# The filler of a double step moved between its two score steps, in the second half of an attention and feed-forward kernel

## The reference, cut to what matters

```python
x = x + layernorm(attn(layernorm(x)))      # x: (16, 2048, 1024), 16 heads of 64
x = x + layernorm(ffn(layernorm(x)))
# attn: q = x@Wq+bq; k = (x@Wk+bk)@Wl+bl; v = (x@Wv+bv)@Wl+bl
#       softmax(q k^T / 8) v, heads joined, @ Wo + bo
# ffn:  x@base_W^T + base_b + shared low-rank pair (16)
#       + 6 routed low-rank pairs (16 each), weighted by a top-2 gate of softmax(x@router_W^T + router_b)
```

## Time and profile before

| | |
|---|---|
| median of the runs of before | 1413.39 us (1412.29 to 1520.67, 3 runs) |
| profiled execution | 1412.82 us |
| its span, slowest core (core 4) | 1411.3 us |
| the other cores' spans | 1407.9 to 1410.2 us |
| mean granted clock of core 4 | 0.989 |
| PE busy | 1317.9 us, 93% of the span |
| ACT busy | 1042.0 us, 74% |
| DVE busy | 705.3 us, 50% |
| POOL busy | 433.5 us, 31% |

### The profile page before, as it was taken

The page is one execution under the profiler, slowest core; times in us unless marked ns, Lnnn a source line. Parts: engine busy times, 40 slices in busy tenths (PEclk is TensorE's granted clock), DMA queues, the critical chain, the costliest instruction groups (busy, mean ns, idle before and its releaser), DMA issues.

```text
span 1411.3 us, 43965 instructions; the slowest of 8 cores (1407.9 to 1411.3 us)
## 1 busy us (share of the span) xinstructions
PE 1317.9 (93%) x17392; PEld 818.0 (58%) x17392; DVE 705.3 (50%) x1679; ACT 1042.0 (74%) x1138; POOL 433.5 (31%) x598
## 2 busy tenths in 40 slices
PE   6899999999999999999998999989999999998883
PEld 2456666666666666665555655555555555555551
DVE  0562434323332323232335676677777667667665
ACT  0367777777777777777777888878888888887651
POOL 5220101000010100000004555555556555465633
PEclk9999999999999999999999999999999999999997
DMA  9950112202020110123852212321222221222011
GB/s 131 232 162 6 54 30 73 64 17 59 15 62 19 47 43 26 25 78 92 113 114 64 77 59 72 121 71 60 77 78 82 91 77 45 86 69 86 23 62 45
DMA packets 67129, 98.90 MB, mean 70 GB/s; under 512 B 30208, under 2 KB 43904, under 8 KB 66416
## 3 DMA queue, kind: packets, MB, share of 16 engines
q1 hardware_dynamic: 56944, 83.03, 19.5%
q0 software_dynamic: 9984, 13.06, 6.8%
HBM read 76.56 MB, written 32.57 MB: 77 GB/s over the span
## 4 chain that ended last, share of the span: by engine, by line
PE 76%; DVE 7%; issue 5%; ACT 5%; DMA 3%; POOL 2%; DVEq 0%; SPq 0%; POOLq 0%; ACTq 0%
PE fb L379 34%; PE sc L1122 17%; PE av L1154 15%; ACT p_sb L1139 4%; PE fb L431 4%; DMA wvT_sb<-wvT 2%; DVE gt L896 1%; PE sc L379 1%; DVE x L812 1%; PE fb L853 1%; DMA xst<-x 1%; PE fb L776 1%; PE sc L1124 1%; POOL wl_sb L67 1%; PE fb L324 1%
## 5 line engine op out<-in xcount | busy, mean ns | idle before, releaser
L1139 ACT ACTIVATE p_sb<-sc 128x1024 bf16<-128x1024 f32 x1024 | 991.0, 1021 | 261.3 <-PE sc L1124 258.2
L1154 PEld LDWEIGHTS av<-v_sb,p_sb 128*128 128x128 bf16 x8192 | 320.8, 97 | 97.1 <-issue 2.3
L1122 PE MATMUL sc<-q_sb,k_sb 64*128 64x256 bf16 (+1 forms) x2176 | 330.6, 265 | 16.0 <-ACT p_sb L1139 14.5
L1154 PE MATMUL av<-v_sb,p_sb 128*128 128x65 bf16 x8192 | 340.1, 193 | 0.5 <-issue 0.5
L1124 PE MATMUL sc<-q_sb,k_sb 64*128 64x256 bf16 (+1 forms) x2176 | 332.8, 266 | 0.0
L1122 PEld LDWEIGHTS sc<-q_sb,k_sb 64*128 64x128 bf16 x2176 | 149.6, 94 | 82.8 <-issue 46.8
L266 POOL TENSOR_SCALAR rsa<-sta 128x1 f32<-128x1 f32 x32 | 7.3, 227 | 523.9 <-DVE sta L261 357.4
L1124 PEld LDWEIGHTS sc<-q_sb,k_sb 64*128 64x128 bf16 x2176 | 146.3, 94 | 0.0
L379 PE MATMUL fb<-wo_sb,ut 128*128 128x512 bf16 x496 | 136.1, 381 | 4.9 <-DVE gt L890 3.3
L379 PE MATMUL fb<-bw_sb,x3fm 128*128 128x512 bf16 x480 | 135.6, 383 | 1.0 <-DVE x3fm L251 0.9
L379 PE MATMUL fb<-xfm,wq_sb 128*128 128x512 bf16 x512 | 129.5, 381 | 0.0
(11 more groups left out here) (172 smaller groups left out, 1478.5 us busy)
## 6 DMA issues: line engine op xcount, KB each, us to landing
xst<-x SPq DMA_DIRECT2D x64, 512.0 KB, 5.2
out<-y_sb SPq DMA_DIRECT2D x31, 512.0 KB, 3.1
urow<-u_scr SPq DMA_DIRECT2D x30, 256.0 KB, 5.2
u_scr<-u SPq DMA_DIRECT2D x64, 64.0 KB, 2.1
q_scr<-kq SPq DMA_DIRECT2D x32, 128.0 KB, 2.5
q_sb<-q_scr SPq DMA_DIRECT2D x4, 1024.0 KB, 8.3
u_scr<-u_sb SPq DMA_DIRECT2D x7, 512.0 KB, 3.6
wkT_sb<-wkT POOLq DMA_DIRECT2D x8, 256.0 KB, 11.6
```

What stands on the lines that cost most here:

```text
L1122: t.matmul(sc[slot][:, ci * w:(ci + 1) * w], k_sb[0:64, j, c * 128:(c + 1) * 128], qa[0:64], start=True, stop=True, tile_position=(0, 0))
L1139: exp_tok[g] = P.op("S", lambda a: a.activation(ps[:], sc[slot][:], AF.Exp, bias=-SHIFT, scale=1.0), tok, av_tok.get(g - 4))
L1154: r = t.matmul(av[u % 2][:, o:o + 65], ps[:, p0:p0 + 128], v_sb[:, j, c * 130 + h * 65:c * 130 + (h + 1) * 65], start=(s == 0 and h == 0 a ...
```

## The change

In the turns of the second half the scores of step 2m+1 are issued after the filler of the turn and ahead of P·V, where before they directly followed those of step 2m. In the first half nothing changes. No instruction is added or taken away; which quanta a turn takes is the same.

```diff
             qk(2 * m)
-            qk(2 * m + 1)
+            if m < NM // 2:
+                qk(2 * m + 1)
             rate = rate_of(m)
             credit = min(credit + rate, 1.6 * rate)
             while filler and credit > 0 and (filler[0][2] is None or filler[0][2]()):
                 credit -= pop()
+            if m >= NM // 2:
+                qk(2 * m + 1)
             if m > 0:
                 pv(2 * m - 2)
                 pv(2 * m - 1)
```

## The result

| | before | after |
|---|---|---|
| median | 1412.84 us | 1432.9 us |
| profiled execution | 1412.82 us | 1432.76 us |
| its slowest core, span | 1411.3 us (core 4) | 1431.2 us (core 5) |
| median span of die 0, die 1 | 1409.0, 1410.1 us | 1429.7, 1427.3 us |

The ratio is 1.0143, 95% interval 1.0129 to 1.0157: +20.1 us where +15.4 us were forecast.

A forecast was written before the change was run, and what follows sets the result against it. TensorE was taken to pace the second half, losing time to scores waiting for ScalarE. Seams of 48.1 us less 32.7 us of waits gave +15.4 us on 1412.82, forecast as 1428 us, 1.1% slower, range 1408 to 1443.

The forecast's parts named there:

- Part 1: Second half: the second score step's wait for ScalarE's exponential goes, 126 places, 32.7 us gained.
- slack of 0.72 us: After the change, the next double step's second scores want their tile 0.72 us after its exponential has freed it.
- Part 2: Second half: two more half-row/full-row passages on TensorE per double step, 0.19 us in each of 253, 48.1 us lost.
- Part 3: Waits of the filler's matmuls, 29.9 us in 26 waits before: net change taken as zero.
- The one example at the loop's start: Passage from filler to scores at 112.02 to 112.33 us, used to price it at 0.31 us, 0.09 us lost.
- the bounds of -6 and +8.8: Limits in us on the change in the filler's waits, by whether their release hangs on earlier filler or on P·V.
- A: Rival: passages cost nothing because scores' weight loads are fetched under the running filler; 1380 us, chance 0.04.
- D: Rival: the scores' wait on ACT comes back behind the filler, so nothing is gained; 1461 us, chance 0.04.
- B: Rival: the filler's waits shrink by half of 29.9 us as turns become more even; 1413 us, chance 0.13.
- C: Rival: VectorE is late for the filler after a unit's end, 24.5 us at most; 1437 to 1453 us, chance 0.12.
- the forecast's case: The main forecast of 1428 us, given as 1417 to 1439 us in the list of chances, chance 0.65.
- What the profile would show: L1122's wait nearly gone, passages 0.31 and 0.21 us, `fb` rows 24 to 39 us, ACT's exponentials standing singly.

The follow-up runs named there:

- both_halves: The changed kernel with the second score step placed behind the filler in the first half too: 1484.7 us, ratio to before 1.0507.

## Why the prediction was right

*Part 1, the wait goes: 32.7 us.* Right in mechanism and size. With exponentials of half length the kernel before falls by 32.7 us, and the tally puts 34.0 us within the scores. The slack of 0.72 us behind the change held: 1.6 us of waits are left, and cheaper exponentials give the changed kernel nothing.

*Part 2, two seams more: 48.1 us.* Right in mechanism, and a little low. Over the first half, where the filler hardly waits, the lines with seams grow by 50.3 us, 0.20 us a turn where 0.19 was said. Between the two kernels with halved exponentials the same five lines go from 233.3 to 278.9 us, 45.6 us; but the line from scores to filler holds the wait of the filler's first matmul too, and it falls by 4.3 us, so the other four give 49.9. The single passages are as priced: in the kernel after the median from a filler matmul of 512 columns to scores is 0.31 us, and from scores to P·V 0.20. The one example at the loop's start was enough to price a passage that occurs nowhere in the second half of the kernel before.

*The term that was missing: P·V itself, 3.3 us.* The prediction took P·V as one block whose inside does not change. From its first start to its last a block of 16 takes 469 ns behind filler and 479 ns behind scores (medians, the same in either half of the loop). The 10 ns lie in the first two distances, on average 29.7 and 33.6 ns before, 38.6 and 35.9 after; the other 13 stay within 0.4 ns. That fits with the weight loads. In the kernel before they start at 903.78, 0.21 us ahead of P·V's 903.99, while filler still runs; in the kernel after they start together with P·V, at 922.73. That this makes the 10 ns is an argument from the two timelines; no run tested it by itself.

```profile
903.78 0.75 PEld L1154 LDWEIGHTS av<-v_sb,p_sb 128*128 128x128 bf16 x16
903.99 0.66 PE L1154 MATMUL av<-v_sb,p_sb 128*128 128x65 bf16 x16
```

Some 2.6 of the 3.3 us are this, and 0.6 us is one wait for the loop's last exponential. All five kernels with P·V behind scores have more within P·V (124.1 to 125.8 us) than those with P·V behind filler (121.1 to 122.4). The rows had a trace of it: 0.67 us behind scores against 0.66.

*Part 3, the filler's waits, taken as zero.* Right. Within the filler the tally has 2.7 us more, from scores to the filler's first matmul 2.0 us less, so +0.7 in all, inside the bounds of -6 and +8.8. The view of the slowest core agrees: its `fb` rows with a releaser sum to 29.7 us in 31 waits, after 29.9 in 26. Within that sum they moved: L853's wait for L812 from 11.3 us in 9 places to 14.4 in 14, L924's for L812 from 7.4 to 5.3, and the two that name the reciprocal from 2.0 to 2.5 us.

*The rivals.* A (seams free) fell by the stops in front of scores and P·V in the first half of `both_halves`, where nothing else changed. D fell with the slack of part 1. B and C asked for the filler's waits to move by some 15 and 12 to 25 us, down or up; they moved by less than 1. That the forecast's case reaches to 1439 us in the list of chances and to 1442 behind the sum is a slip that changes nothing.

*What the profile would show.* Right on L1122's wait, on the passages, on 0.21 us in front of L1154 and on the sum of the `fb` rows; nor did the stretch's end fall into the lower clock for longer (0.98 from 1294 to 1387 us, after 0.96). Wrong on ACT: the exponentials do not stand singly, but in twos that belong to neighbouring turns, since the next turn's first scores are ready before a late second exponential ends.

*The sum.* 48.1 - 32.7 = 15.4 was forecast. By the terms as measured it is 50 of seams + 3.3 of P·V + 0.7 of the filler - 34.0 of waits = 20.0, against the 19.9 of the tally and the 20.1 of the timing. The 4.6 us between are the P·V term that was missing and 1.9 us of seams, less 1.3 us by which the wait was put too low.

## What to carry to other kernels

Count in the queue how often neighbouring matmuls pass from part of the array's rows to all of them or back, and price each passage from starts of matmuls in the trace before splitting a block: here a wait of 0.26 us in half of the turns was traded for 0.20 us of seams in all of them. A split that removes a wait belongs only where the wait is larger than the seams: here 15 of them, after the shortest turns, gave as much as 103. And when a wait is named for one engine, make that engine's work cheaper in both orders: the pair of runs gives the wait and the price of the new order separately.

## What the runs showed of the hardware that was not expected

A passage between half-row and full-row matmuls costs 0.10 us in either direction (0.20 us where the next pair of scores comes after 0.11, and 0.31 where the next filler matmul comes after 0.22), and somewhat more than the gap that one sees at it: the 16 matmuls of P·V took 10 ns longer behind scores than behind filler, 479 against 469 ns. The stop stands in the profile as idle time of the weight loads with no releaser and hardly at all as idle time of the matmuls. An exponential over 128x512 takes 594 ns and one over 128x1024 1021 ns. A straight line through these two sizes, which is an estimate, has (1021 - 594) / 512 = 0.83 ns for each column and some 167 ns beside it; by it two halves would take 1.19 us.
